# A third raw-weight buffer in the attention stage, and moved statistics, loads and sums in the FFN stage

## What is computed

```
x = layernorm(x + mixer(x))              # down-projection, two state-space layers, up-projection
x = layernorm(x + xattn(x, ctx))         # 16 heads, 1601 keys per batch, latent size 64
x = layernorm(x + ffn(x))

# xattn
C_q, C_kv = x @ Wq_d, ctx @ Wkv_d
scores = einsum('bnhl,bkl->bhnk', (C_q @ W_qk).reshape(b, n, 16, 64), C_kv) / 8
out = einsum('bhnk,bkhd->bnhd', softmax(scores), (C_kv @ Wv_u).reshape(b, nkv, 16, 64))

# ffn: int weights, one scale and one zero per group of 128 rows
W = (int_weight - repeat(zeros, 128)) * repeat(scales, 128)     # gate, up: 1024 x 3584, down: 3584 x 1024
y = (silu(x @ W_gate) * (x @ W_up)) @ W_down
```

## Time and profile before

| what | value |
|---|---|
| median of 3 runs | 2720.79 us (2718.92 to 2731.97) |
| the profiled execution, own time | 2725.14 us |
| its span, first to last instruction | 2721.3 us, mean granted TensorE clock 0.987 |
| PE busy / PEld busy | 2598.3 us (95%) / 1982.2 us (73%) |
| DVE busy | 2274.3 us (84%) |
| ACT busy | 1651.3 us (61%) |
| POOL busy | 2078.3 us (76%) |
| transfers | 420.64 MB, mean 155 GB/s |

### The profile page before, as it was taken

The page is one execution under the profiler, slowest core; times in us unless marked ns, Lnnn a source line. Parts: engine busy times, 40 slices in busy tenths (PEclk is TensorE's granted clock), DMA queues, the critical chain, the costliest instruction groups (busy, mean ns, idle before and its releaser), DMA issues.

```text
span 2721.3 us, 42088 instructions
## 1 busy us (share of the span) xinstructions
PE 2598.3 (95%) x14328; PEld 1982.2 (73%) x14328; DVE 2274.3 (84%) x2602; ACT 1651.3 (61%) x2588; POOL 2078.3 (76%) x1597
## 2 busy tenths in 40 slices
PE   7998899999999999999988999999999999999997
PEld 4665667777666766676666888888888888788885
DVE  2765688888988898899857999899998899899988
ACT  3454587887777777787755554444455555555553
POOL 1002389889898989888957999999887888888883
PEclk9899999999999999999989999999999999999999
DMA  7426677877777677877772222222213222232222
GB/s 278 167 92 202 213 216 229 231 221 205 230 235 243 203 229 224 246 222 230 223 242 79 100 93 86 70 71 77 76 64 124 78 85 78 70 120 81 79 93 77
DMA packets 166792, 420.64 MB, mean 155 GB/s; under 512 B 30130, under 2 KB 57652, under 8 KB 166068
## 3 DMA queue, kind: packets, MB, share of 16 engines
q1 hardware_dynamic: 164276, 409.57, 48.2%
q10 hardware_dynamic: 2304, 8.39, 0.8%
HBM read 248.43 MB, written 75.04 MB: 119 GB/s over the span
## 4 chain that ended last, share of the span: by engine, by line
PE 48%; POOL 5%; SPq 4%; ACT 2%; DVE 2%; issue 2%; DMA 1%; POOLq 0%; ACTq 0%; DVEq 0%
PE c_ps L1625 43%; SPq L914 3%; PE b_po L1040 2%; PE b_sc L1021 2%; POOL b_pt L1319 1%; POOL b_rw L1370 1%; PE c_ps L1637 1%; POOL shared L1319 1%; ACT b_pr L1107 1%; PE b_mi L1050 0%; POOL b_rw L1372 0%; DVE c_sum_g L1781 0%; POOL b_qs L1328 0%; DVE c_stats L1841 0%; POOL c_sum_g L1866 0%
## 5 line engine op out<-in xcount | busy, mean ns | idle before, releaser
L1781 DVE SCALAR_TENSOR_TENSOR c_acc<-c_ps,c_sd,c_acc 128x1024 f32<-128x1024 f32 x440 | 562.7, 1281 | 92.3 <-PE c_ps L1625 91.6
L1683 ACT ACTIVATE c_scaled<-c_ps,c_sgu 128x1024 f32<-128x1024 f32 x336 | 375.1, 1117 | 422.1 <-PE c_ps L1625 417.5
L1107 ACT ACTIVATE b_pr<-b_sc,b_nm 128x799 f32<-128x799 f32 (+1 forms) x512 | 477.1, 933 | 176.5 <-DVE b_pr L1196 158.1
L1866 POOL TENSOR_TENSOR c_sum_u<-c_sum_u,c_scaled 128x1024 f32<-128x1024 f32 x168 | 404.5, 2408 | 100.4 <-ACT c_scaled L1683 98.9
L1866 POOL TENSOR_TENSOR c_sum_g<-c_sum_g,c_scaled 128x1024 f32<-128x1024 f32 x168 | 404.7, 2409 | 72.7 <-ACT c_scaled L1683 71.7
L1021 PE MATMUL b_sc<-b_kh,b_qs 128*128 128x402 f32 (+1 forms) x1024 | 397.1, 388 | 35.9 <-ACT b_pr L1107 29.7
L1203 DVE STREAM_TRANSPOSE b_tn<-b_pr 128x1280 f32<-128x1280 f32 x256 | 385.4, 1506 | 39.0 <-DMA b_pt<-b_tn 12.3
L1021 PE MATMUL b_sc<-b_kl,b_qs 128*128 128x402 f32 (+1 forms) x1024 | 356.1, 348 | 0.0
L1319 POOL COPY b_pt<-b_tn 32x640 f32<-32x640 f32 x430 | 306.8, 713 | 53.2 <-DVE b_tn L1203 23.6
L1781 DVE SCALAR_TENSOR_TENSOR c_sum_g<-c_ps,c_sgu,c_sum_g 128x1024 f32<-128x1024 f32 x224 | 286.2, 1278 | 25.6 <-PE c_ps L1625 20.0
L1185 DVE TENSOR_REDUCE b_nm_first<-b_sc 128x1 f32<-128x802 f32 x256 | 250.9, 980 | 63.9 <-PE b_sc L1021 60.2
(11 more groups left out here) (215 smaller groups left out, 4930.4 us busy)
## 6 DMA issues: line engine op xcount, KB each, us to landing
b_pt<-b_tn SPq DMA_DIRECT2D x774, 80.0 KB, 2.8
shared<-b_tn SPq DMA_DIRECT2D x378, 80.0 KB, 2.7
c_uw_int<-wint_u SPq DMA_DIRECT2D x56, 512.0 KB, 3.5
c_gw_int<-wint_g SPq DMA_DIRECT2D x56, 512.0 KB, 3.4
c_dw_int<-wint_d SPq DMA_DIRECT2D x56, 512.0 KB, 3.4
a_cx<-in_b_ctxT SPq DMA_DIRECT2D x16, 1608.0 KB, 10.0
b_rw<-in_c_gw SPq DMA_DIRECT2D x28, 512.0 KB, 4.2
b_rz<-in_c_gz SPq DMA_DIRECT2D x28, 512.0 KB, 5.6
```

The costliest lines, as they stand in the source:

```text
L1107: S.activation(pr[u % 2][:, k0:k1], sc[:, at + lo:at + hi], ACT.Exp, bias=nm[:, u % 2:u % 2 + 1], accum_out=den[:, g % 2, q, half:half + 1 ...
L1683: S.activation(dst[:, :], pair[SLOT[x, t] % 4][:, :], ACT.Identity, scale=scale(x, t)).then_inc(s_e, 1)
L1781: V.scalar_tensor_tensor(out=total, in0=pair[SLOT[x, t] % 4][:, :], scalar=scale(x, t), in1=before, op0=ALU.mult, op1=ALU.add).then_inc(s_ ...
L1866: G.tensor_tensor(total, total, scaled[m % 2][:, :], ALU.add).then_inc(s_add, 1)
```

## The change

What it does, by stage:

- *Everywhere in the mixer and at its end*: some semaphores are merged into one, and the counts that are waited for rise accordingly (first into xin[0], gates into s_soft, xmid into s_prep, e1 and decay_in into one, the two of the attention's weights into one). No instruction moves. This part is left out below.
- *Attention*: three raw buffers instead of two. The new first one lies in the array `shared` behind the keys, where later c_gw_int0 and c_uw_int0 lie. Three blocks are loaded in front of the first exchange instead of one. In a pair the order is now exchange, load, store: the load is that of block `block_of(p - 2) + 3`, the store that of `block_of(p - 1)`. A key load is cut in its two halves, in two following pairs. In the last batch the pair without a block is the 31st instead of the 30th of 32.
- *Into the FFN*: the first u and g weights are loaded at the pairs 29 and 30 of the last batch, counted from 0 at pair 96 (125 and 126 of all), behind the last store from raw buffer 0; the rows of x2 are loaded in the pairs 28 to 31 (124 to 127); identity and scales after pair 125. The last batch's statistics are spread over four steps of period 0, two of a row tile each, and the four tail events come earlier by one place each.
- *The end of the FFN*: in period 56 the last two gate products, g6 and g7, stand before u2 and d0 in the order. Four sums (d7 of block 53, d6 of 54, d1 and d3 of 55) are scaled by ScalarE and added by GpSimd.
- *The last layer normalisation*: the reciprocal of the tile before stands between a tile's statistics and its variance, the shift between the variance and the small addition.

```diff
-KEYS_LOAD = {24: 2, 52: 3}
+KEYS_LOAD = {24: (2, 0), 25: (2, 1), 52: (3, 0), 53: (3, 1)}
...
-FREE = (1, 2, 5, 9, 13, 17, 21, 23, 25, 29, 31)
+FREE = [(1, 2, 5, 9, 13, 17, 21, 23, 25, 29, 31)] * (L - 1) + [(1, 2, 5, 9, 13, 17, 21, 23, 25, 30, 31)]
...
+RAW = 3
...
-        rw = [sb(f"b_rw{j}", [P, HID], I32) for j in range(2)]
-        rz = [sb(f"b_rz{j}", [P, HID], I32) for j in range(2)]
+        rw = [sb(f"b_rw{j}", [P, HID], I32) for j in range(RAW - 1)]
+        rz = [sb(f"b_rz{j}", [P, HID], I32) for j in range(RAW - 1)]
+        raw_at = keys_end + NB
+        rw.insert(0, shared[:, raw_at:raw_at + HID].bitcast(I32))
+        rz.insert(0, shared[:, raw_at + HID:raw_at + 2 * HID].bitcast(I32))
...
-                if i >= 2:
-                    Q.wait_ge(s_wout[i % 2], 16 * (i // 2))
-                Q.dma_start(rw[i % 2][:, :], raw[n + "w"][j, :, :]).then_inc(s_rin[i % 2], 16)
-                if i >= 2:
-                    Q.wait_ge(s_sub, i - 1)
...
+                if i >= RAW:
+                    Q.wait_ge(s_wout[i % RAW], 16 * (i // RAW))
+                Q.dma_start(rw[i % RAW][:, :], raw[n + "w"][j, :, :]).then_inc(s_rin[i % RAW], 16)
+                if i >= RAW:
+                    Q.wait_ge(s_sub, i - RAW + 1)
...
-            load_keys(1)
-            load(0)
+            for z in range(2):
+                load_keys(1, z)
+            for i in range(RAW):
+                load(i)
...
             def pair(p):
+                exchange(p)
+                i = block_of(p - 2) if p >= 2 else None
+                if i is not None and i + RAW < len(BLOCKS):
+                    load(i + RAW)
                 if p and block_of(p - 1) is not None:
                     store(block_of(p - 1))
-                exchange(p)
-                i = block_of(p)
-                if i is not None and i + 1 < len(BLOCKS):
-                    load(i + 1)
                 if p in KEYS_LOAD:
...
+FIRST_PAIR = 29
+ROWS_AT = {28: (0,), 29: (1, 2), 30: (3, 4, 6), 31: (7, 5)}
...
-for n, when in enumerate(((0, 22), (1, 0), (1, 3), (1, 5))):
+for n, when in enumerate(((0, 16), (0, 22), (1, 0), (1, 3))):
     EXTRA.setdefault(when, []).append(("tail", 0, n))
+for q, when in enumerate(((0, 1), (0, 1), (0, 4), (0, 10))):
+    EXTRA.setdefault(when, []).append(("last", 0, q))
...
+SHARED_D = [("d7", NT2 - 3), ("d6", NT2 - 2), ("d1", NT2 - 1), ("d3", NT2 - 1)]
+LAST_STEPS = [(x, lag) for x, lag in STEPS if x in ("u0", "d6", "g4", "u1", "d7", "g5")] + \
+             [(x, lag) for x, lag in STEPS if x in ("g6", "g7")] + \
+             [(x, lag) for x, lag in STEPS if x not in ("u0", "d6", "g4", "u1", "d7", "g5", "g6", "g7")]
...
-        for n, (x, lag) in enumerate(STEPS):
+        for n, (x, lag) in enumerate(LAST_STEPS if p == NT2 else STEPS):
...
             def early(p):
                 n = p - LATE
-                if 2 <= n < 2 + len(FIRST):
-                    load(*FIRST[n - 2])
...
+                if FIRST_PAIR <= n < FIRST_PAIR + len(FIRST):
+                    Q.wait_ge(b['wout'][0], 16 * len(BLOCKS) // RAW)
+                    load(*FIRST[n - FIRST_PAIR])
+                for t in ROWS_AT.get(n, ()):
+                    if t < QT:
+                        Q.wait_ge(b['stored'][0], 16 * QT * 2)
+                    elif t < QT + 2:
+                        Q.wait_ge(b['wout'][t - QT + 1], 16 * len(BLOCKS) // RAW)
+                    else:
+                        Q.wait_ge(b['sub'], len(BLOCKS) - HT + t + 1)
+                    load_rows(0, t)
+                if p == PAIRS - 3:
...
+            def evict_sum(j):
+                x, t = SHARED_D[j]
+                m = NT2 * len(ADDED) + j
+                S.wait_ge(s_add, m - 1)
+                S.wait_ge(s_p["d"], t * KC + int(x[1]) + 1)
+                S.activation(scaled[m % 2][:, :], pair[SLOT[x, t] % 4][:, :], ACT.Identity, scale=scale(x, t)).then_inc(s_e, 1)
...
+            def add_sum(j):
+                x, t = SHARED_D[j]
+                k = int(x[1])
+                m = NT2 * len(ADDED) + j
+                G.wait_ge(s_add, m)
+                G.wait_ge(s_e, NT2 * len(EVICTED) + j + 1)
+                summed(G, t - 1, k)
+                G.tensor_tensor(acc[:, k, :], acc[:, k, :], scaled[m % 2][:, :], ALU.add).then_inc(s_add, 1)
...
+                if t:
+                    o = (t - 1) % OR
+                    V.wait_ge(s_std, 2 + t)
+                    V.reciprocal(rstd[:, o:o + 1], rstd[:, o:o + 1]).then_inc(s_own, 1)
...
+                if t:
+                    V.wait_ge(s_own, inverted)
+                    V.scalar_tensor_tensor(out=nmr[:, o:o + 1], in0=mv[:, o, 0:1], scalar=-1.0, in1=rstd[:, o:o + 1],
+                                           op0=ALU.mult, op1=ALU.mult).then_inc(s_nmr, 1)
```

More of the change, by code:

```diff
@@ L403, in scalar @@
         def scalar():
-            S.wait_ge(first, 32)
             for l in range(L):
@@ L788 @@
 PER_BATCH = len(BLOCKS) // L
-FREE = (1, 2, 5, 9, 13, 17, 21, 23, 25, 29, 31)
+FREE = [(1, 2, 5, 9, 13, 17, 21, 23, 25, 29, 31)] * (L - 1) + [(1, 2, 5, 9, 13, 17, 21, 23, 25, 30, 31)]
 LATE = 3 * (PAIRS // L)
-BUSY = [n for n in range(PAIRS // L) if n not in FREE]
+BUSY = [[n for n in range(PAIRS // L) if n not in free] for free in FREE]
 LN_SLOTS = [15, 16, 19, 20, 23, 24, 27, 28]
@@ L845, in attention @@
         s_root = sem("root")
-        s_rin, s_sub, s_cast = [sem("raw0"), sem("raw1")], sem("sub"), sem("cast")
-        s_wout = [sem("wint0"), sem("wint1")]
+        s_rin, s_sub, s_cast = [sem(f"raw{j}") for j in range(RAW)], sem("sub"), sem("cast")
+        s_wout = [sem(f"wint{j}") for j in range(RAW)]
         keys = keys_of(shared)
@@ L1288, in vector, with last_statistics, last_variance @@
                     norm_piece(k)
-            def last_statistics():
-                for q in range(QT):
-                    for c in range(2):
-                        statistics(L - 1, q, c)
+            def last_statistics(q):
+                for c in range(2):
+                    statistics(L - 1, q, c)
+            def last_variance():
                 variance(L - 1)
@@ L1819, in vector @@
                     statistics(e[2])
+                elif e[0] == "last":
+                    rest["last_statistics"](e[2])
                 elif e == ("tail", 0, 0):
-                    rest["last_statistics"]()
+                    rest["last_variance"]()
                 elif e == ("tail", 0, 2):
```

153 lines of the change are left out of this document (78 added, 75 removed).

## The result

The changed kernel takes 2707.16 us (median of 6 runs, 2705.70 to 2712.36), the kernel before 2723.09 (6 runs, three more than stood ahead). The ratio is 0.9949, with an interval of 0.9935 to 0.9963: faster by about half a per cent, just at the bound that the prediction set for "can be told". The forecast was 2699, the range 2685 to 2716. So the direction and the range held, and the gain came out at 16 us where 21.7 were forecast. Of the 8 us between 2699 and 2707, 2.3 are the higher median of the kernel before, the rest is the smaller gain.

The account below looks back on a forecast made before the run. TensorE was taken as full in attention and steady FFN, so only stalls could move. Terms -14 + 5.1 - 1.5 - 5 - 4.3 - 2.0 = -21.7 against the median 2720.79 gave 2699 us, range 2685 to 2716.

Parts of the forecast that it names:

- Interior: 61 attention heads: third raw buffer, earlier loads and exchange before store remove stalls, -14 us (bounds -28 to 0).
- I take half: Attention heads: -14 chosen between 0 and -28, as one late instance was SP and the other bytes in the queue.
- Start: Before the first head: two more raw blocks, 2.1 MB, in front of exchange 0, +5.1 us (bounds +1 to +7.9).
- Last pairs: End of attention: more issues before the last two exchanges, against no identity wait, -1.5 us (bounds -2.7 to +5.9).
- FFN's start: Attention to FFN: spread statistics remove TensorE's 3.88 us gap and its lower clock, -5 us (bounds -8 to -2).
- the factor: FFN's start: four-column VectorE instruction, held 2.21 us beside GpSimd's addition; called the same form as 0.16 in the tail.
- Last sums and tail: FFN's end: reordered g products and shared sums, -4.3 us; last normalisation's reciprocal and shift moved into gaps, -2.0 us.
- (a): Attention heads: GpSimd takes SP's place as what holds VectorE; interior gives 7, time 2706 us; chance 0.22.
- (d): Attention heads: the third buffer does nothing, stores cast late again, time 2713 us; chance 0.10.
- (c): Attention: all interior stalls go and the last pairs gain their 2.7, time 2684 us; chance 0.10.
- (b): Start, interior, last pairs: bytes in the one queue make exchanges land late, +5.5 us, 2726; chance 0.08.
- The sign for (b): VectorE's transposes still waiting over 20 us in all for landings would show bytes in the queue as the bound.

Follow-up runs that it names:

- run 3: Changed kernel with three raw buffers, but the store again in front of the exchange: 2720.39 us, ratio 0.9992; 61 heads 1016.5 us.
- run 1: Changed kernel with only raw block 0 in front of the first exchange, blocks 1 and 2 behind exchanges 0 and 1: 2701.88 us, ratio 0.9933.
- run 2: Changed kernel with first u and g weights and FFN rows 4 and 6 loaded behind the last exchange: 2701.77 us, ratio 0.9924.
- run 9: Changed kernel with one block before the first exchange, second-batch rows behind exchanges 5 to 8, FFN rows spread earlier, weights behind the last exchange: 2689.44 us, ratio 0.9878.
- run 4: Changed kernel with the last batch's eight statistics in one lump and tail events at old steps: FFN's start 66.05 us instead of 60.35.
- run 8: Changed kernel with the last layer normalisation in its old order: eight tiles 15.4 us instead of 13.9, stretch to the end 21.86 instead of 20.65.

## Why the prediction was right or wrong

**Interior: right.** -16.0 against -14. SP's waits in front of stores and GpSimd's waits for blocks fell as named, and run 3 shows the mechanism: the order of the pair (10.4 us) on top of the third buffer with its earlier loads (5.6). "I take half" was a guess between bounds; that it came so near is luck, since the reason given for it, one late instance by SP and one by bytes, says nothing of the sizes. Still open is the rest: the 61 heads stand 12.7 us over 986.4 and the 7.0 of the turned keys, though hardly an exchange begins late. TensorE's waits in these heads sum to 16.9 us (28.7 before), 14.2 of them in 41 waits for ScalarE's exponentials (22.7 in 51 before). The one wait for a landing that is left, 1.26 us near 1127, is for an exchange that was issued behind a block's two transfers, a store and a row of x1. No run took these away.

**Start: right.** +5.8, and 6.1 back in run 1, against +5.1 from 2.1 MB at 408 GB/s. The mechanism was the one named, the landing of exchange 0 behind bytes.

**Last pairs: wrong, and this is the step that failed.** The prediction counted seven more issues in front of the last two exchanges at 0.56 us (+2.2, +1.7; by the trace they are eight), set -2.66 for the identity against them, and took -1.5 "since TensorE's chain there waits mostly for its own predecessors". The wait for the identity did go, and yet the profile showed +5.8: what stands against the 2.66 came to 8.5 us and not to 1.2. The six other profiles that leave the last loads where they are have 25.6 to 31.1 us, so +3.5 to +9. The reason given failed: TensorE waited there for the landings, 4.79 and 1.68 us, and in runs 2 and 9 the loss goes with the loads. Two things were left out. The delays add up, since exchange 127 stands behind all that exchange 126 does: 3.4 and then 5.8 us. And behind the wait TensorE worked at the lower clock, in this profile for most of 18 us; 6.7 of the 10.8 us that run 9 takes back are this, less in other executions. The prediction had charged just that to the old gap in the FFN, "4 us x 0.4", and left it out here. Its upper bound of +5.9 has no working behind it, so that +5.8 still lies within is luck.

**FFN's start: the mechanism was right and the size too small.** -8.5 against -5. The lump was worth 5.7 by run 4, near the 5.5 of the working. The other 2.8 were put at nothing: the first turns no longer run at the lower clock. They are not the 2.66 of the identity, which end at the first turn and so lie in the last pairs. Of the factor, the 0.16 that the prediction sets beside 2.21 is a form of one column and not of four.

**Last sums and tail: right, both a little less.** -3.3 against -4.3: the last eight products came 2.1 us earlier in place of 2.4, and VectorE ended 2.3 us behind TensorE instead of 1.7. The tiles gave 1.57 of the 2.0, and the end of the span 1.2.

**The sum.** That 2707 lies well inside the range is in part luck: the 7.3 us of the last pairs were partly paid for by the FFN's start (-3.5) and the interior (-2.0).

**Rivals.** (a) GpSimd as the bound, and (d), a third buffer that does nothing, fall with 1006.1 us. (c) fails twice: the interior gave 16 of its 28, and the last pairs grew. (b) bytes in the one queue was right at one of its three places, the start (5.8 of its 7.9), and wrong for the interior. In the last pairs its price came true (5.8 of 5.9), its cause only in part. The traces part the two: counted from their transposes, exchanges 126 and 127 landed 3.0 and 7.5 us later than before, and 1.6 and 5.5 of that had passed before SP began to issue them. So there most of it is SP's time for the transfers in front, and the rest slower issue and landing. At the start exchange 0 was issued at once, and all of it is the landing. The Trainium skill (DMA: Bandwidth & Descriptors, Queues, rings and completion order) says that each engine consumes a ring's descriptors in order; runs 1 and 9 agree. (One queue holds from the attention on; in the mixer ScalarE issues the 16 stores of x1 itself, the last at 310 us.)

**The sign for (b)** was badly set: "over 20 us" of VectorE's transposes waiting for landings is more than the kernel before had (19.6).

## What to carry to other kernels

Where one queue carries small transfers that an engine waits for and bulk that nobody needs yet, the order of issue decides: here the bulk cost 6 us in front of the first exchange and 9 to 14 in front of the last two, and nothing that could be seen once it was moved behind the first exchanges or spread over earlier pairs. Put wholly behind the last exchange it came late for the next stage. A further buffer and a better order can each be worth little alone and much together, so test both halves. Where an edit makes TensorE wait some microseconds, look at the granted clock behind the wait: here it stood at the lower level for 7 to 17 us of the last pairs, in profiles of kernels with the same loads there. So give such a term wide bounds.

## What the runs showed that was not expected

The end of the mixer, which no run touched, moved between 325.1 and 336.9 us from one profile to another. That is as much as most edits here are worth, and it is why stretches from mark to mark tell more than whole times. And the last sums took 23.8 us in most profiles but 25.4 in two that had the same code there: in these two the granted clock was at its lower level for 3.4 us within the last eight products (from 2670.4 in run 1, from 2683.0 in run 8), behind the same wait of 1.7 us for the last hidden block that the others have at full clock.
